# Sums of squares by one-column products: whole 128-column weight loads against two 64-column halves per row block

## The reference

```
g = y * silu(gate)                        # tokens x 8192 channels
gg = g.reshape(b, s, G, INTER // G)       # G = 8 groups of 1024 channels
var = mean(gg * gg, axis=-1)              # one number per token and group
gg = gg * rsqrt(var + EPS)
out = gg.reshape(b, s, INTER) * norm_w
return einsum('bsi,oi->bso', out, out_proj_w)
```

## Time and profile before

| | |
|---|---|
| three runs | 1772.48, 1772.05, 1772.44 us (median 1772.44) |
| the profiled execution | 1772.93 us, of which 1771.1 us is the span from the first instruction to the last |
| mean granted TensorE clock | 0.992 of full |
| TensorE busy | 97% of the span |
| VectorE, GpSimd, ScalarE busy | 71%, 68%, 48% |
| 16 DMA engines | 20.4% busy with the kernel's own queue, 61 GB/s |

### The profile page before, as it was taken

How to read it: one execution, slowest core, us unless ns; L and a number is a source line. 1 busy time by engine, 2 the same in 40 slices (tenths; PEclk the granted TensorE clock), 3 DMA queues, 4 the chain that set the end, 5 groups by cost and what they waited for, 6 DMA issues and landing times. The chain is left out here.

```text
span 1771.1 us, 34371 instructions
## 1 busy us (share of the span) xinstructions
PE 1723.5 (97%) x10392; PEld 1414.7 (80%) x10392; DVE 1259.9 (71%) x1892; ACT 845.1 (48%) x1273; POOL 1200.7 (68%) x873
## 2 busy tenths in 40 slices
PE   6899999999999999999999999999999989999998
PEld 5688888888888888888888888888888878788886
DVE  7888548863887288728873788368846875877776
ACT  4666346633664366536652665256535652222221
POOL 3499659964897489757985798469956987523430
PEclk9999999999999999999999999999999999999999
DMA  3333013211231123103320222022202311111101
GB/s 100 96 81 90 25 49 88 88 29 42 79 91 42 30 79 90 54 22 87 85 59 18 73 90 72 18 68 83 84 18 61 85 44 60 48 36 48 47 13 48
DMA packets 71342, 107.23 MB, mean 61 GB/s; under 512 B 16741, under 2 KB 25061, under 8 KB 71305
## 3 DMA queue, kind: packets, MB, share of 16 engines
q1 hardware_dynamic: 70296, 105.38, 20.4%
q10 hardware_dynamic: 1008, 1.38, 0.3%
HBM read 103.51 MB, written 3.15 MB: 60 GB/s over the span
## 5 line engine op out<-in xcount | busy, mean ns | idle before, releaser
L795 PE MATMUL proj<-xhi,w_hi 128*128 128x512 f32 x1072 | 431.8, 403 | 5.9 <-DVE gate L1119 5.9
L797 PE MATMUL proj<-xhi,w_lo 128*128 128x512 f32 x1072 | 418.8, 391 | 0.0
L796 PE MATMUL proj<-xlo,w_hi 128*128 128x512 f32 x1072 | 418.5, 390 | 0.0
L492 POOL TENSOR_TENSOR g_lo<-gated,g_hi 128x512 fp32r<-128x512 f32 x128 | 164.1, 1284 | 198.1 <-ACT g_hi L724 198.0
L1100 DVE SCALAR_TENSOR_TENSOR v<-proj,par_sb,v 128x510 f32<-128x510 f32 x378 | 275.0, 741 | 20.8 <-DVE v L1100 9.7
L795 PEld LDWEIGHTS proj<-xhi,w_hi 128*128 128x128 f32 x1072 | 201.3, 188 | 65.1 <-issue 13.9
L467 POOL TENSOR_TENSOR gated<-hs,gate 128x512 f32 (+1 forms) x128 | 191.0, 1513 | 71.7 <-DVE hs L1225 71.7
L797 PEld LDWEIGHTS proj<-xhi,w_lo 128*128 128x128 f32 x1072 | 201.2, 188 | 43.0
L796 PEld LDWEIGHTS proj<-xlo,w_hi 128*128 128x128 f32 x1072 | 201.6, 188 | 37.8
L427 POOL TENSOR_TENSOR w_lo<-w_raw,w_hi 128x512 fp32r<-128x512 f32 x144 | 182.0, 1283 | 60.9 <-ACT w_hi L568 60.9
L590 ACT ACTIVATE v<-proj,par_sb 128x512 f32<-128x512 f32 x126 | 98.2, 780 | 238.8 <-PE proj L797 238.8
(11 more groups left out here) (178 smaller groups left out, 3323.0 us busy)
## 6 DMA issues: line engine op xcount, KB each, us to landing
w_raw<-in_win SPq DMA_DIRECT2D x144, 256.0 KB, 2.7
fade_l<-faded SPq DMA_DIRECT2D x128, 256.0 KB, 3.3
wo_raw<-in_wout SPq DMA_DIRECT2D x64, 256.0 KB, 2.7
M<-in_w SPq DMA_DIRECT2D x14, 512.0 KB, 3.8
row_r<-rows SPq DMA_DIRECT2D x256, 3.0 KB
row_l<-rows SPq DMA_DIRECT2D x256, 3.0 KB
cb<-in_w SPq DMA_DIRECT2D x7, 512.0 KB, 3.5
out<-resid SPq DMA_DIRECT2D x8, 256.0 KB, 2.0
```

What stands on the lines that cost most here:

```text
L795: e.matmul(o, hi_l, hi_r, start=first, stop=False)
L796: e.matmul(o, hi_l, lo_r, start=False, stop=False)
L797: return e.matmul(o, lo_l, hi_r, start=False, stop=last)
```

## The change

Each row block's sums are made by two products in place of one. Each takes 64 of the 128 columns of the block as weights and writes to the 64 partitions of `misc` that belong to them, so the two lie on the two column halves of the array. Inputs, waits and the single semaphore increment (on the last product) are as before, and so is everything else in the kernel.

```diff
                 pe.wait_ge(sacc.sem, sacc.window(g, 0))
                 for t in range(TT):
-                    mm = e.matmul(misc[:, t:t + 1], sqacc[:, t * P:(t + 1) * P], ones[:, :], start=True, stop=True)
+                    for half in range(2):
+                        first = t * P + half * HD
+                        mm = e.matmul(misc[half * HD:(half + 1) * HD, t:t + 1], sqacc[:, first:first + HD], ones[:, :],
+                                      start=True, stop=True)
                 mm.then_inc(varr.sem, 1)
```

## The result

Eleven runs of the changed kernel have a median of 1777.81 us, from 1774.90 to 1790.97; the kernel before, eleven runs beside them, 1772.54 us, from 1771.85 to 1773.57. The ratio is 1.0036, with a 95% interval of 1.0023 to 1.0049: slower, by a third of a percent, outside the range given, and with a spread that the kernel before doesn't have. The profiled execution took 1776.94 us, 1775.0 of it span.

What follows compares the result with a forecast made beforehand. TensorE was taken as the bound (busy 1723.5 of 1771.1 us). +0.30 per window hidden in seven windows and +0.2 in the last put the profiled 1772.93 at 1773.1, a median of 1772.6 us; range 1771.2 to 1774.9.

Steps and rivals of the forecast that it cites:

- rival B: L963's narrow loads cost as much as wide ones when one column moves: some +11 us, 1784; chance 6%.
- The price of a pass: Each L963 pass with a 64-column load takes 0.055 us, half of today's 0.106, judged from L932's pace.
- Rival A: Loads on the two column halves run beside each other, a pair costing one narrow load: 1771.0 to 1771.7 us; chance 13%.
- The sum for one window: From projection to L977: entering halves, 31 passes and leaving make 2.23 us against 1.93, so +0.30.
- The drains: Changing between whole array and halves around L963 drains TensorE twice per window: 0.32 us entering, 0.20 leaving.
- The cover: In the first seven windows TensorE's later wait for g_lo hides the +0.30, and would hide any gain; 0.73 us free.
- Rival C: The wait for g_lo isn't independent of L963, so the seven windows each pay: +2.4 us, 1774.8; chance 6%.
- The last window: Exposed, at 1.2 GHz: L963 to L977 takes 3.52 to 3.73 us against 3.40; +0.2 us taken.

Runs made afterwards that it cites:

- e2: Changed kernel with 16 more TensorE instructions (long-satisfied waits) ahead of the group loop; 1770.3 us, ratio 0.9986.
- e11: e2 with the order turned round, all row blocks on one column half, then all on the other; 1772.56 us, ratio 0.9998.
- e12: e2 with four products of 32 columns per row block, on the four column quarters; 1770.99 us, ratio 0.9986.
- e4: Changed kernel with halves for the first four row blocks only, the other four's sums left out, loop of old length; 1770.44 us, ratio 0.9984.
- e7: Changed kernel with halves in the last window alone, whole 128-column products in the loop's seven windows; 1771.17 us, ratio 0.9989.
- e10: Changed kernel with 8 more TensorE instructions (waits) ahead of the group loop; 1770.66 us, ratio 0.9988.
- e8: Kernel before with 16 more TensorE instructions (waits) ahead of the group loop, nothing else; 1774.05 us, ratio 1.0005.
- e6: Changed kernel with 64 more TensorE instructions (waits) inside the group loop and 16 ahead of it; 1811.01 us, ratio 1.0220.
- e5: Changed kernel with 64 more TensorE instructions (waits behind product 4) inside the group loop; 1851.73 us, ratio 1.0442.
- e1: The changed kernel again, unaltered, for a second profile and more runs; 1776.96 us, ratio 1.0016 against the kernel before.
- e9: Changed kernel with 2 more TensorE instructions (waits) ahead of the group loop; 1778.33 us, ratio 1.0025.
- e3: Kernel before, whole 128-column products, with 32 more TensorE instructions (waits behind product 4) inside the loop; 1784.05 us, ratio 1.0063.

## Why the prediction was wrong

**The step that failed** is the sentence "Nothing else moves: the single increment still stands on the last product, the same two waits stand ahead, no DMA and no other engine's instruction is touched." A DMA was touched: the one that brings TensorE its program. The change adds 32 instructions to a loop whose seven blocks just fitted, with its start a few instructions ahead of a block's end. I priced every added instruction by the time it runs and none by the room it takes. No rival was about code either, so the range ended at 1774.9 with nothing beyond it but rival B, which didn't happen. The price is about 7 us a stall, mostly one in a run. With it the changed kernel lies at 1777.8 us; without it, in e2, at 1770.3.

**The price of a pass** was mis-sized: 0.055 us taken, 0.029 measured. For a load alone 0.055 was near enough: passes that stay on one half start 0.058 apart in e11. What was wrong is that loads on alternating halves were taken to follow one another. L932, which alternates too, could not show it: I wrote that 0.055 "is what the load costs or less", and took the upper end, though L932 moves 128 columns in each pass and L963 one. Rival A, at 13%, is what happened: "The halves load beside each other". Of the two pages weighed there, "TensorEngine Tiling (Array Packing)" of the Trainium skill, section "Key Properties", with tiles that load and multiply in parallel, is the one that e11 and e12 agree with, for one-column products. The sum for one window, 2.23 us, measured 1.35.

**The drains** were right in the main: 0.32 us into the halves as forecast, and 0.13 out of them (201.05 less the last pass at 200.92), where 0.20 was taken from L932.

**The cover** was right, and it decides what the change could bring: product 2 starts 8.21 us behind the projection against 8.25, in seven windows. Rival C falls. Rival B falls with the pass price.

**The last window**: forecast +0.2 us, with rival A's price -1.4 or half of that. e2 has it without a stall; TensorE in order of time, against the earlier trace rows:

```profile
1462.48 1.87 PE L967 MATMUL decay<-ones,sqacc 128*64 128x1 f32 x32 [5.55 <-POOL sqacc L482]
1464.28 0.79 PE L982 MATMUL y<-wo_hi,g_hi 128*128 128x512 f32 x1
```

1.80 us in place of 3.40. The clock returns at 1469.3 as it did in the earlier trace rows, so the products behind it, at 1.2 GHz, use up half: lined up with the kernel before, e2 is 0.1 us ahead just before this window, 1.8 ahead at its L982 and 0.9 once the clock is back. That is 0.8 us for the window in this profile. Taken from 1450 to 1472 us, so that the stretch at 1.2 GHz ahead of the window is counted too, e2, e4, e7, e10 and e12 gain 0.4 to 0.7. But e8, with whole products, loses 1.5 there against the same kernel before, since its clock returns later: where the low stretches fall moves the time by more than the gain.

The medians of e2, e4, e7, e10 and e12 lie 1.9 to 3.1 us under the kernel before. Most of the rest lies, in e2's profile, at the very end. The kernel before does its last products at clock 0.50, from 1762.8 us on (shown above). e2 does them at full clock:

```profile
1760.00:1768.40 8.40, 3.47 (x14) 2.37 (x14) 3.02 (x7) 0.37 (x1) 0.00 (x0) 1.00 0.26 96
```

There its lead grows from 0.9 us at 1761 to 2.5 at the last product. The low stretch near 1524 us, which the kernel before has and e2 has not, is worth nothing: the 1.3 us that it brings are waited away by 1535. e8's profile has no low stretch at the end either, and gains the same 1.6 us there without any halves. So this part belongs to the clock; why it should favour the kernels with a short last window in the medians was not settled.

**What is argued and not shown:** how the eighth block does it. The likely way is that TensorE, when it enters a block, has the next one fetched. In seven blocks that makes eight with the one ahead, which is all that the memory holds; in eight it makes nine, and the one thrown out holds the loop's first instructions. The packets agree. The last one of the first turn comes at 226 us in the kernel before, whose loop reaches far into its seventh block, and at 240 to 245 in e2, e6, e10, e11 and e12, whose seventh block begins near the loop's end, and then no more come in the loop; and the nine of the changed kernel are eight blocks and one ahead, the first two 0.3 us apart (792.9 and 793.2). If the jump back comes 8 instructions into the block, the fetch mostly has not begun (by the steps in the times, 23 stalls in 23 runs of six jumps each, about one jump in six); 72 instructions in, it always has (e5). The runs show the place, the depth and the packets; that a block is thrown out, and which, is inferred.

The better kernel than either is any of e2, e7, e10: faster than the kernel before by 0.11 to 0.14%, which is less than the 0.2% that I called measurable, though the intervals exclude 1. The simplest that doesn't hang on where code lies is e7, which changes only the window that stands outside the loop: its loop of 1517 instructions fits in seven blocks of 256 wherever it begins (255 + 1517 is less than 7 x 256 = 1792), the one of 1549 only if it begins early enough in a block.

## What to carry to other kernels

An instruction added to a loop costs room as well as time. Where a hardware loop is nearly as long as the engine's instruction memory, count its instructions and the blocks that it touches, and look at the page's "instruction" queue: packets there in the later turns of a loop, with idle time put down to "issue" at a turn's start, are a loop that fetches itself anew. A run time that comes in steps of equal size is worth a look at that queue.

Products that move one column are paid by their weight loads. Split over column groups and issued in turn, they took half the time on two halves and less than a third on four quarters (112 ns for 128 columns, 58 and 33); but the gain counts only where the products' end is waited for, here in one window of eight.

## What the runs showed of the hardware

- TensorE's loop of 1549 instructions runs from memory in seven blocks of 256 (e2, e10: 20 and 19 packets) and loses itself by chance in eight (e1, e9: 28 packets); six instructions ahead of the loop (e9, e10) change the median from 1778.3 to 1770.7 us.
- One loss costs 6.8 us (e5 less e6, six jumps), of which 3.6 is idle time; in the profiles of the changed kernel, e1 and e9 the idle time is 4.2 to 4.5. The rest is the stretch at 1.2 GHz that follows.
- One-column products with f32 weights, from start to start: 128 columns 0.112 us; 64 columns 0.058 on one column half, and 0.058 for two on both halves; 32 columns 0.033 for four on the four quarters.
- Satisfied waits in TensorE's stream cost 0.62 us for 32 instructions (e3) and 5.6 us for 64 at the same place (e6), 3.8 of it idle and the rest at the lower clock.
